# Splitting keys and queries into three bf16 parts: GpSimd alone, or ScalarE for the rounding and GpSimd for the differences

## What is computed

```python
# layer 0; layer 1 is the same without _apply_rope
q = (query @ Wq.T + bq).reshape(B, S, H, D).transpose(0, 2, 1, 3)   # H = 16 heads, D = 8
k = (key @ Wk.T + bk).reshape(B, S, H, D).transpose(0, 2, 1, 3)
q = _apply_rope(q, cos, sin)
k = _apply_rope(k, cos, sin)
scores = jnp.einsum('bhsd,bhtd->bhst', q, k) / math.sqrt(D)
attn = jax.nn.softmax(scores, axis=-1)
out = jnp.einsum('bhst,bhtd->bhsd', attn, v)
return out @ Wo.T + bo
```

## Time and profile before

| | us |
|---|---|
| median of 3 runs | 1698.57 |
| lowest, highest | 1696.36, 1701.63 |
| the profiled execution | 1698.44 |
| its span | 1696.6 |
| main loop of the attention, layer 0, begins | 51.9 |
| main loop of the attention, layer 1, begins | 432.2 |

### The profile page before, as it was taken

The page is one execution under the profiler, slowest core; times in us unless marked ns, Lnnn a source line. Parts: engine busy times, 40 slices in busy tenths (PEclk is TensorE's granted clock), DMA queues, the critical chain, the costliest instruction groups (busy, mean ns, idle before and its releaser), DMA issues. The chain is left out here.

```text
span 1696.6 us, 26265 instructions
## 1 busy us (share of the span) xinstructions
PE 1404.4 (83%) x8869; PEld 885.2 (52%) x8869; DVE 872.2 (51%) x2507; ACT 553.5 (33%) x1291; POOL 417.1 (25%) x729
## 2 busy tenths in 40 slices
PE   4788886994798875886888599473999999999998
PEld 2566663552576763564787377352444444444443
DVE  4576645874564643342455343474445555555525
ACT  1456554651565651222444133141011011011001
POOL 2666711102755501000244322541000000000000
PEclk8699987995788987998667699796999999999999
DMA  6676750004667528500010111231122112202200
GB/s 163 196 161 150 165 120 1 1 1 114 146 162 152 153 36 350 220 0 19 13 32 18 36 53 50 56 114 70 72 93 106 66 41 106 75 32 105 78 28 13
DMA packets 134175, 151.38 MB, mean 89 GB/s; under 512 B 12150, under 2 KB 117942, under 8 KB 128806
## 3 DMA queue, kind: packets, MB, share of 16 engines
q1 hardware_dynamic: 127494, 142.28, 28.7%
q0 software_dynamic: 3296, 6.76, 1.3%
q10 hardware_dynamic: 3264, 0.79, 0.2%
HBM read 99.33 MB, written 49.48 MB: 88 GB/s over the span
## 5 line engine op out<-in xcount | busy, mean ns | idle before, releaser
L2694 DVE TENSOR_TENSOR l3f_weighted_T<-l3f_w_e,l3f_xnT 128x512 f32<-128x512 f32 x128 | 88.3, 691 | 129.6 <-PE psum L2445 115.1
L2445 PE MATMUL psum<-l3f_weighted_T,w_l3f_q 128*128 128x512 f32 x256 | 133.7, 604 | 16.4 <-DVE l3f_weighted_T L2694 14.6
L2445 PE MATMUL psum<-l3f_weighted_T,w_l3f_k 128*128 128x512 f32 x256 | 131.6, 596 | 0.0
L2445 PE MATMUL psum<-l3f_weighted_T,w_l3f_v 128*128 128x512 f32 x256 | 131.4, 595 | 0.0
L710 DVE TENSOR_REDUCE l1x_minus_max<-psum 128x4 f32<-128x512 f32 x128 | 86.0, 687 | 88.1 <-PE psum L373 87.2
L2454 PE MATMUL psum<-l3f_weighted_T,w_l3f_o 128*128 128x512 f32 x256 | 124.4, 624 | 1.7 <-DVE l3f_weighted_T L2694 1.7
L2694 DVE TENSOR_TENSOR l3f_weighted_T<-l3f_w_e,l3f_oT 128x512 f32<-128x512 f32 x128 | 88.4, 692 | 57.2 <-PE psum L2454 30.5
L710 DVE TENSOR_REDUCE l0x_minus_max<-psum 128x4 f32<-128x512 f32 x128 | 85.4, 686 | 57.2 <-PE psum L373 56.5
L531 ACT ACTIVATE l0x_probsT<-psum 128x512 f32<-128x512 f32 x128 | 73.9, 594 | 52.6 <-PE psum L386 43.7
L111 POOL TENSOR_TENSOR l3f_ln_rstd<-l3f_ln_mean_var,eps 128x4 f32<-128x4 f32 x8 | 1.9, 243 | 355.5 <-DVE l3f_ln_mean_var L104 355.5
L531 ACT ACTIVATE l1x_probsT<-psum 128x512 f32<-128x512 f32 x128 | 73.8, 594 | 40.4 <-PE psum L386 31.3
(11 more groups left out here) (486 smaller groups left out, 3004.1 us busy)
## 6 DMA issues: line engine op xcount, KB each, us to landing
l3f_w_e<-l3f_weights_scratch SPq DMA_DIRECT2D x32, 1024.0 KB, 4.6
sorted_x<-zeros SPq DMA_DIRECT2D x1, 16896.0 KB, 59.2
l0x_k_scratch<-l0x_k_parts SPq DMA_DIRECT2D x24, 384.0 KB, 4.0
l0x_k_stack<-l0x_k_scratch SPq DMA_DIRECT2D x16, 576.0 KB
l0x_q_stack<-l0x_q_scratch SPq DMA_DIRECT2D x48, 192.0 KB
l1x_k_scratch<-l1x_k_parts SPq DMA_DIRECT2D x24, 384.0 KB, 5.5
l1x_k_stack<-l1x_k_scratch SPq DMA_DIRECT2D x16, 576.0 KB
l1x_q_stack<-l1x_q_scratch SPq DMA_DIRECT2D x48, 192.0 KB
```

Source lines behind the costliest of these rows:

```text
L2445: ins = pe.matmul(bank[:, :], w[name][:, e, :], xe[:, e % 2, :], start=(e == 0), stop=(e == NE3 - 1))
L2694: dve.tensor_tensor(xe[:, e % 2, :], wE[:, g % 2, e, :], src, ALU.mult).then_inc(s_xe, 1)
```

## The change

The change divides `split` between two engines. ScalarE gets `first_cast` and `second_cast`, a copy of a float32 tile of SBUF into a bf16 tile, for the first and the second part. GpSimd keeps the rotary sum (`whole`), the remainder (`first_rest_of`) and the third part (`last_part`). The remainder tile `rest` becomes two tiles, `k_rest` and `q_rest`. New semaphores hand the work to and fro: `s_whole` (sum ready), `s_cast` (a part rounded), `s_rest` (remainder ready).

The pieces stand in the main loop as follows. Keys: `whole` and `first_rest_of` in c = 1 on GpSimd, with `first_cast` at the end of c = 1 on ScalarE; `second_cast` in the middle of c = 2 on ScalarE, `last_part` in c = 2 on GpSimd. Queries: `whole`, and after the keys' last part `first_rest_of`, in c = 2, with `first_cast` at the end of c = 2 on ScalarE; `second_cast` in the middle of c = 3, `last_part` in c = 3 after `moments`. For group 1, ahead of the loop, both splits stand one behind the other before the first `split_max`. Group 0 stays on VectorE.

```diff
--- before.py
+++ after.py
@@ -188,7 +188,7 @@
         gb = sb("tanh_g_bias", [P, P], F32)
         turned = {n: [sb(f"{n}_turned{i}", [P, T], F32) for i in range(2)] for n in "kq"} if rope else None
         full = {n: sb(f"{n}_full", [P, T], F32) for n in "kq"}
-        rest = sb("rest", [P, T], F32)
+        rests = {n: sb(f"{n}_rest", [P, T], F32) for n in "kq"}
         first_full = {n: sb(f"{n}_first_full", [P, T], F32) if rope else full[n] for n in "kq"}
         first_rest = sb("first_rest", [P, T], F32)
         parts = {n: sb(f"{n}_parts", [P, NPART, T], BF16) for n in "kq"}
@@ -227,7 +227,9 @@
         s_vout = sem("v_ready")
         s_parts = {n: sem(f"{n}_split") for n in "kq"}
         s_first = sem("first_split_step")
-        s_split = sem("split_step")
+        s_whole = {n: sem(f"{n}_turned_sum") for n in "kq"}
+        s_cast = {n: sem(f"{n}_parts_cast") for n in "kq"}
+        s_rest = {n: sem(f"{n}_rest_ready") for n in "kq"}
         s_stored = {n: sem(f"{n}_parts_in_dram") for n in "kq"}
         s_stack = {n: [[sem(f"{n}_stack_in_{p}_{hf}") for hf in range(2)] for p in range(2)] for n in "kq"}
         s_S = sem("scores_in_psum")
@@ -508,6 +510,18 @@
                     act.wait_ge(s_proj["q"], g)
                 act.activation(xnT[:, :], bankP1[:, :], ACT.Copy).then_inc(s_xnT, 1)
 
+            def first_cast(n, g):
+                if rope:
+                    act.wait_ge(s_whole[n], g)
+                else:
+                    act.wait_ge(s_out[n], g + 1)
+                parts_stored(act, n, g - 1)
+                act.activation(parts[n][:, 0, :], full[n][:, :], ACT.Copy).then_inc(s_cast[n], 1)
+
+            def second_cast(n, g):
+                act.wait_ge(s_rest[n], g)
+                act.activation(parts[n][:, 1, :], rests[n][:, :], ACT.Copy).then_inc(s_cast[n], 1)
+
             def v_out(g):
                 act.wait_ge(s_proj["v"], g + 1)
                 if g >= 3:
@@ -549,6 +563,11 @@
                 normalise_x(g)
                 xnT_out(g)
                 evacuate("q", g)
+                if g == 1:
+                    first_cast("k", 1)
+                    second_cast("k", 1)
+                    first_cast("q", 1)
+                    second_cast("q", 1)
                 v_out(g)
             for j in range(LEAD - 1):
                 max_out(j)
@@ -570,12 +589,20 @@
                     aT_out(j - 2)
                 if j + 2 < NSEQ:
                     max_out(j + 2)
+                if c == 2 and ahead is not None:
+                    second_cast("k", ahead)
+                if c == 3 and ahead is not None:
+                    second_cast("q", ahead)
                 if j < NSEQ:
                     exps(j, 2)
                 if j + 2 < NSEQ:
                     max_rows(j + 2)
                 if j < NSEQ:
                     exps(j, 3)
+                if c == 1 and ahead is not None:
+                    first_cast("k", ahead)
+                if c == 2 and ahead is not None:
+                    first_cast("q", ahead)
                 if ahead is not None:
                     if c == 0:
                         evacuate("k", ahead)
@@ -590,7 +617,7 @@
         def _(pool):
             pool.memset(v1[:, :, :, :, :], 1.0).then_inc(s_fill, 1)
             pool.memset(zeros[:, :], 0.0).then_inc(s_fill, 1)
-            step, max_step = Chain(pool, s_split, 0, 0), Chain(pool, s_mstep, 0, 0)
+            max_step = Chain(pool, s_mstep, 0, 0)
             rstd_step = Chain(pool, s_rstd, 0, 0)
 
             def moments(g):
@@ -609,17 +636,22 @@
                 xs = k.x_sb[:, rows(g)].rearrange("p (c d) -> p c d", c=GS)
                 pool.tensor_tensor(xs, xs, bcast(gb[:, :].unsqueeze(1), [P, GS, P]), ALU.add).then_inc(s_xb, 1)
 
-            def split(n, g):
+            def whole(n, g):
                 pool.wait_ge(s_out[n], g + 1)
                 if rope:
-                    step(pool.tensor_tensor(full[n][:, :], turned[n][0][:, :], turned[n][1][:, :], ALU.add))
-                parts_stored(pool, n, g - 1)
-                p = [parts[n][:, a, :] for a in range(NPART)]
-                step(pool.tensor_tensor(p[0], full[n][:, :], bcast(k.ones[:, 0:1], [P, T]), ALU.mult))
-                step(pool.tensor_tensor(rest[:, :], full[n][:, :], p[0], ALU.subtract))
-                step(pool.tensor_tensor(p[1], rest[:, :], bcast(k.ones[:, 0:1], [P, T]), ALU.mult))
-                pool.tensor_tensor(p[2], rest[:, :], p[1], ALU.subtract).then_inc(s_parts[n], 1)
-                pool.wait_ge(s_parts[n], g + 1)
+                    pool.wait_ge(s_cast[n], 2 * (g - 1))
+                    pool.tensor_tensor(full[n][:, :], turned[n][0][:, :], turned[n][1][:, :], ALU.add)\
+                        .then_inc(s_whole[n], 1)
+
+            def first_rest_of(n, g):
+                pool.wait_ge(s_cast[n], 2 * g - 1)
+                pool.tensor_tensor(rests[n][:, :], full[n][:, :], parts[n][:, 0, :], ALU.subtract).then_inc(s_rest[n], 1)
+
+            def last_part(n, g):
+                pool.wait_ge(s_cast[n], 2 * g)
+                pool.wait_ge(s_rest[n], g)
+                pool.tensor_tensor(parts[n][:, 2, :], rests[n][:, :], parts[n][:, 1, :], ALU.subtract)\
+                    .then_inc(s_parts[n], 1)
 
             def split_max(j):
                 pool.wait_ge(s_max, 4 * j + 4)
@@ -635,9 +667,11 @@
             pool.wait_ge(s_fill, 4)
             for g in range(2):
                 moments(g)
-            split("k", 1)
+            for n in "kq":
+                whole(n, 1)
+                first_rest_of(n, 1)
+                last_part(n, 1)
             split_max(0)
-            split("q", 1)
             split_max(1)
             moments(2)
             for g in range(2):
@@ -651,11 +685,16 @@
                 if c == 0 and ahead is not None:
                     add_bias(ahead)
                 if c == 1 and ahead is not None:
-                    split("k", ahead)
+                    whole("k", ahead)
+                    first_rest_of("k", ahead)
                 if c == 2 and ahead is not None:
-                    split("q", ahead)
+                    whole("q", ahead)
+                    last_part("k", ahead)
+                    first_rest_of("q", ahead)
                 if c == 3 and t + 3 < NG:
                     moments(t + 3)
+                if c == 3 and ahead is not None:
+                    last_part("q", ahead)
 
         @block.vector
         def _(dve):
```

## The result

| | before | after |
|---|---|---|
| median, us | 1698.57 | 1780.42 |
| lowest to highest (5 runs each) | 1688.83 to 1701.63 | 1769.55 to 1791.83 |
| profiled execution | 1698.44 | 1769.55 |

After / before is 1.0485 [1.0450, 1.0519], 82 us slower; 1782 was forecast. The profiled execution of after is its fastest, so its parts add up to 71 us.

What follows compares the result with a forecast made beforehand. Bound: the chain after Q (end of the query projection): query split, store, landing, load, landing, first scores, with TensorE idle. 1698.4 + 44 (layer 0, including 2 for slow clock) + 40 (layer 1) = 1782 us; range 1745 to 1804.

Steps and rivals of the forecast that it cites:

- The link of the chain: Group-closing chain, layers 0 and 1: any delay of the query parts lengthens the group by the same amount.
- The growth of the chain: From query projection's end to next first scores in layer 0: 24.3 us, against 20.7 before.
- some 5 us: TensorE's idle time in each group, as its own work ends before the stack arrives.
- The clock: TensorE at 1.2 GHz after each wait: first scores to projection's end 8.9 us instead of 5.25, layer 0; 7.96, layer 1.
- some 2.85 for the projection, half of it slow: Layer 0's query projection after the wait: 2.85 of the 8.9 us from first scores to its end.
- The costs put at nothing: ScalarE's added roundings, having room at 15.3 of 25 us busy, and group 1's split ahead of the loop: no cost.
- L399's 4.1 us: TensorE's waits for GpSimd's split_max in layer 0, six groups; their removal worth nothing while the stack is late.
- Clock high in layer 0: Rival: TensorE keeps full clock in layer 0, group 29.6 us, layer +24; 1762 us; chance 0.14.
- Chain grows less: Rival: shorter landings (-12), no slow clock in half the groups (-10 a layer at most); about 1750 us; chance 0.09.
- Dear roundings: Rival: ScalarE's roundings are dear, or its delayed exponentials hold TensorE; 1797 us; chance 0.10.
- Nothing happens: Rival: the group's slack takes the 3.6 us; 1698 us; chance 0.02.
- The transfers bound and not the parts: Rival: late stack transfers hide the later parts, TensorE gains up to 4 us a layer; 1691 us; chance 0.03.

Runs made afterwards that it cites:

- e11: Kernel before, with only the query store of groups 2 to 6 held back until the next moments is done; 1700.34 us, 0.9980.
- e3: Changed kernel, with the query store ahead of the key load in SyncE's list; 1755.04 us, 1.0294 to the kernel before.
- e1: Kernel before, GpSimd still doing all split steps but at the change's places, no rounding on ScalarE; 1770.28 us, 1.0351.
- e2: Kernel before, plus four unread 128x512 casts a group on ScalarE at the change's places; 1702.45 us, 0.9988.
- e7: Changed kernel's division of work, but all key steps in pass c = 1 and all query steps in c = 2; 1710.90 us, 1.0080 to before.
- e8: Changed division, key steps in c = 1 and query steps in c = 2, plus query store ahead of key load; 1697.23 us, 1.0002 to before.
- e6: Changed kernel, plus 24 unread bf16 matmuls on TensorE ahead of each group's wait for the stack, from group 2; 1767.35 us, 1.0403 to before.
- e5: Changed kernel, with query store ahead of key load and the queries' last part ahead of moments; 1727.95 us, 1.0162 to before.
- e9: Kernel before, with only the query store put ahead of the key load in SyncE's list; 1692.73 us, 0.9929.
- e4: Changed kernel, with the queries' last part ahead of moments on GpSimd; 1772.91 us, 1.0384 to the kernel before.

## Why the prediction came out right, and where it was wrong

**The time, right; the group, nearly.** 1782 us was forecast and 1780.42 measured; a group of 33.2 in layer 0, and (260.50 - 98.84) / 5 = 32.3 found, from group 2's first scores to group 7's.

**The engines' steps, right.** In the group shown: keys' first rounding Q - 0.4 forecast, Q - 0.7 found; rotary sum of the queries 3.3 and 2.95; keys' second rounding 4.7 and 4.55; keys' last part 5.9 and 5.8; queries' last part 12.1 and 11.4. Both roundings take 0.62 us (0.63 taken from the earlier trace rows).

**The link of the chain, wrong.** The step "any delay of the query parts beyond nothing lengthens the group by the same amount" failed: `e11` delayed their store by 2.5 to 2.8 us at no cost. The row had SyncE waiting for the query parts, and I took the last one waited for as the one that sets the end. But the store lands only behind the key load that was issued ahead of it; of those 5.86 us in the earlier trace rows the store alone takes 2.5 (`e3`), and the load the rest. The delay that counts here is the keys'. The prediction worked out that path too (stored at Q + 5.9, landed 5.4 later) and used it only to find SyncE free for the query store, at the same Q + 12.1. It did not see that the stack's landing has to be counted from there.

**The growth of the chain, too small.** 3.6 us was forecast (20.7 to 24.3). Measured over the groups of layer 0 it is 20.1 to 25.5 on average, +5.4. The key load moved from Q + 5.95 to Q + 11.5 on average over the six groups, 5.55, which would explain all of it. Even the keys' path as it was worked out would have given only 4.6 (stored at Q + 5.9, was Q + 1.3 in the earlier trace rows): the group shown has the latest keys of its layer. Over the six groups before stored them at Q + 0.0 on average, after at Q + 5.7. One group was taken for all. So TensorE waits longer than the "some 5 us" forecast: 6.0 to 9.1 in groups 2 to 7 of both layers.

**The clock, too dear.** From first scores to Q 8.9 us was forecast for layer 0, and 7.0 found (5.25 before): 1.8 instead of 3.65 a group. The slow stretch ends within 5 us of the wait's end, before the projection, which therefore is not slow. The term that was too large is "some 2.85 for the projection, half of it slow". It is not too large for a kernel that waits about as long as was forecast: `e1`, with waits of 4.7 to 6.3 us, needs 8.4 to 9.7 in layer 0, and its projection takes 2.7 to 3.6 instead of 1.88. In after the clock falls 2.8 to 5.6 us ahead of the first scores of these groups, so part of the slow time passes in the wait. In layer 1, 7.96 was taken for every group and holds for every other one (5.93, 7.97, 6.00, 7.96, 5.95). All six first scores of layer 0's groups in after take 0.58 or 0.59 and not 0.38. With that the rule cited from the Trainium skill ("TensorE: Matmul & The Clock Gate", section "HAM oscillation — how this bites in real kernels"), that each pass then starts on the slow clock, this trace agrees; what that costs a group was my estimate, and too high for this kernel.

**The sum.** In layer 0 the two errors, 1.8 us a group too little and 1.9 too much, cancel: +40.6 where +42 was forecast. In layer 1 they do not quite: +33.9 instead of +40, with groups of 32.2 instead of 33.4. So the time is right in part by luck: two sizes were wrong in opposite directions, and the way was the keys' and not the queries'. The two errors may hang together, as a longer wait can take in more of the slow time; no run varies one of them alone.

**The costs put at nothing, right.** ScalarE's load (`e2`: 0.9988). Group 1's split ahead of the loop: group 2's Q is at 72.09 where it was 72.75. L399's 4.1 us have gone, and bring nothing, as TensorE waits for the stack. GpSimd's 61 us less busy time (417.1 to 356.1) bring nothing here either: `e1`, without that relief, is not the slower one.

**The rivals.** Clock high in layer 0: no, but half true, for its projection. Chain grows less: no, it grew more. Dear roundings: no, 0.62. Nothing happens: no. The transfers bound and not the parts: its reason was right, its side wrong. The queries' path is indeed held by a transfer, but by one that starts with the keys' parts, and the change delays those as well. Its point of decision, SyncE not waiting for GpSimd, should have been asked of each of the two tiles.

**My later expectations** failed where they rested on the same step: `e11`, and `e7` and `e8`, of which I expected gains because the queries came early enough. `e6` failed by the dear clock. `e5` came out at the ratio expected, but by the clock and not by earlier parts.

## What to carry to other kernels

The last thing waited for is not yet the thing that sets the end: ask how long its successor would take alone, and if it takes longer in the program, what is in the queue ahead of it. Splitting a chain of small steps over two engines costs each step the place where the other engine's list is ready for it; here the same division of work was worth +4.9% at one set of places, and -1.4% at another with one pair of DMA issues swapped, a swap that alone is worth -0.7% (`e9`). A slow clock costs only where the engine would have worked: two short waits with the slow stretch between them (`e5`) were 25 us cheaper here than one wait with the slow stretch behind it (`e3`). A wait that an edit removes has to be sought elsewhere before the edit is believed (`e4`).

## What the runs showed of the hardware

- A 384 KB store to DRAM landed within 2.5 us (`e3`), 2.8 (`e9`) and 3.4 (`e11`, 3.8 us behind the issue of the load), and 5.9 and 6.4 in before and after, 1.9 and 0.9 us behind the issue of a 576 KB load on the same queue.
- In after, behind waits of 6 to 9 us, TensorE's slow stretch of 1.2 GHz ended before the next query projection in all groups of layer 0 from group 2 on and in every other group of layer 1; in `e1`, behind waits of 4.7 to 6.3 us, it took in part or all of that projection in layer 0. What decides is open; the length of the wait alone does not (6.36 in after, 6.29 in `e1`).
- 24 bf16 matmuls put in front of a wait kept TensorE at 2.4 GHz at the first scores behind it in all six groups of layer 0 and four of six in layer 1 (`e6`: 0.38 instead of 0.58).
- In layer 0 of after the keys' stores need 4.8 to 5.0 and 6.6 to 6.8 us by turns until the key load goes out. Why was not found.
